# DVE's sorting step cut in two: the rows' places first, the blocks' experts and biases as a step of their own

## The chip, the cores and the metric

The kernel runs on one core of one Trainium2 chip. The metric is device microseconds (us) of one execution, lower is better. A core has five engines with a queue of instructions each: PE (matrix products), DVE (vector work), ACT (activations and copies), POOL (here it issues indirect DMAs, one for each 128 rows) and SP (here it issues all other DMAs). An engine runs its instructions in order, and engines meet in semaphores: an instruction that waits holds up all that stand behind it on its engine.

## The reference

Eight graphs of 1024 nodes with 128 features pass four residual layers, each behind a layer norm:

```python
x = x + _L0_gnn_ref(adj, _layernorm(x), W, b)         # maximum over up to 25 neighbours, then a product
x = x + _L0_ffn_ref(_layernorm(x), ...)               # 8 experts of width 512, the best 2 of each node
x = x + _L1_gnn_ref(_layernorm(x), adj, ...)          # masked attention, 8 heads of 16
x = x + _L1_ffn_ref(_layernorm(x), ...)               # 6 experts, the best 2 of each node

gate_logits = xf @ Wg + bg                            # _L0_ffn_ref, the layer that the change touches
top_w, top_i = jax.lax.top_k(gate_logits, 2)
top_w = softmax(top_w)
for e in range(E):
    h = gelu(xf @ W1[e] + b1[e])
    out = out + w_dense[:, e:e + 1] * (h @ W2[e] + b2[e])
```

## The kernel before

**Passes.** The kernel is a software pipeline over graphs. A pass works on up to four graphs at once, each in another stage: `att` (attention over keys and values, and the second expert layer) on graph g, `unit` (scores of the attention) on g+1, `near` (the neighbour product and the first expert layer) on g+2, `load` (finding and gathering neighbours) on g+3, and the loading and norm of g+4. Passes run from g = -4 to 7; the passes g = 0 to 3 are one loop and have all five parts, pass 4 has all but the last, pass 5 has no `load`.

**Order.** Each pass is planned at build time by `schedule`: steps such as `("dest",)` or `("find", 2)` stand in threads (`chain`), wait for others (`gate`), and cost what the table `COURSE` says. The planner takes the step that can start first and writes one list; each engine then runs its part of each step in the order of that list. So a changed cost or a new step can move steps of every engine.

**The sorting step.** In `near`, each node's two best experts are found on DVE (step `cha 0`, function `two_best`), PE counts ranks (`rank`), and DVE's step `dest` (function `places`, L1137) turns ranks into the place of each row in an order sorted by expert (`dest`, written at L1164), and then works out which expert each of 23 blocks of 128 sorted rows belongs to (`block_at`, L1169 to L1173) and each block's first biases (`bias_of`, a view of the tile `mparts`, L1174 to L1184). The semaphore `bk` is raised by the last of them, at L1182. POOL's step `scatter` waits for `bk` at L924 and then issues 16 indirect DMAs (L930) that write rows of `xn` to their places in `xs_dram`; POOL goes on with the neighbour gathers of later tiles (`gather t`, L903). SP then loads the sorted rows (`xs`, into a part of `HB`), and PE runs the blocks (`xT`, `up`, `ut`, `dn`); `up` reads `block_at`, ACT's part of `ut` reads `bias_of`.

**Steps around it, in a loop pass.** On DVE: `chb 0` (weights of the two experts, L1200 to L1207, written to `wts`), `pmax 0` (maximum over gathered neighbours in `G`, L1053 to L1070), `wc 0` (copies the transposed weights to `WT`, L1216), `find 2` (neighbour indices of tile 2, L1021 to L1037), `fina 0 1` (copies a finished attention product to `tmp`, L1366), `ba 0` (adds the second bias, L1226), `mask 0` (L1331), `finc 0 1` (L1373, L1375). On PE: `st` (scores with the mask, L1691 and L1694) and `av` (values, L1705) alternate, ACT's exponential (L1491) lies between them; `wt 0` (L1604) needs `wts`, `b 0` (L1614) needs `WT`, `finb 0 1` (L1715) needs `tmp` of `fina 0 1`. Later on PE and DVE: `s t h`, the score maxima of the next graph (PE L1670, DVE L1337). SP's step `stack 0` (L855) loads twelve slices of 128 KB once the attention step `st 1 0 7` is done; `load_adj` (L835) brings a tile of the adjacency matrix to `adj_sb`, which `deg` on ACT (L1409), `class` on PE (L1543) and `find` on DVE read.

Of the kernel before, what the change touches and what calls it, by code (L numbers as in the profile page):

```python
# [68 lines left out]
    "finb": [("PE", 0.5)], "finc": [("DVE", 0.9)], "projt": [("PE", 0.5), ("ACT", 0.6)], "projm": [("PE", 1.0)],  # L69
# [4 lines left out]
    "ye": [("ACT", 0.7)], "ys": [("SP", 5.0)], "scatter": [("POOL", 24.0)], "collect": [("POOL", 12.0)],  # L74
    "mix": [("DVE", 2.4)], "load_x": [("SP", 14.0)], "again": [("SP", 6.0)], "store_x": [("SP", 4.0)], "load_adj": [("SP", 5.0)],
# [42 lines left out]
def planned(att, unit, near, load, ahead):  # L118

    p = Plan()  # L120
# [24 lines left out]
    if near:  # L145
        if not unit:
            p.threads.append([("bias",)])
            p.gate(("gT",), ("bias",))
        p.chain([("gT",), ("gnn",), ("gnn_add",), ("lnv", 1), ("sq", 1), ("ln", 1), ("t0",), ("lg0",), ("cha", 0),
                 ("ex", 0), ("chb", 0), ("wt", 0), ("wc", 0), ("b", 0), ("ba", 0)])  # L150
        p.chain([("cha", 0), ("rank",), ("dest",)])
        p.threads[-1].pop(0)
        p.gate(("chb", 0), ("dest",))
        p.threads.append([("load_res",)])
        p.gate(("load_res",), ("take",) if unit else None)
        p.gate(("gnn_add",), ("load_res",))
# [88 lines left out]
    if near:  # L245
# [12 lines left out]
        blocks = [("xT", 0)]  # L258
# [95 lines left out]
def signals(step):  # L354

    k = step[0]
# [69 lines left out]
        return A("rank") + [("mk", ("cha", 0), 1)]  # L426
    if k == "dest":
        return [("bk", step, 1)]
    if k == "xs":
        return [(f"xl{step[1] % 2}", step, 16)] + ([("sca", ("scatter",), 16 * 2 * TILES)] if step[1] == 0 else [])  # L430
    if k in ("xT", "up", "ut"):
# [66 lines left out]
def graph_kernel(nc, x, adj, gW, gb, Wg, bg, W1, b1, W2, b2, Wq, Wk, Wv, Wo, bo,  # L498
                 rw1, rb1, rw2, rb2, ew1, eb1, ew2, eb2, ew3, eb3, out):
    ctx = ExitStack()  # L500
    with ctx:
# [3 lines left out]
        def sem(name):  # L505
# [32 lines left out]
        dest = sb("dest", [P, 2, TILES], U32)  # L538
        block_at = sb("block_at", [1, QUADS * HTILES], I32)
        counts = [sb(f"counts{i}", [P, EP]) for i in range(3)]  # L540
# [105 lines left out]
            "dg": "degree_excess_ready", "cat": "degree_class_ready", "aggr": "aggregate_ready", "q1": "first_part_ready",  # L646
            "parts": "parts_ready", "pd": "parts_stored", "stack0": "stacks_loaded0", "stack1": "stacks_loaded1",
            "dl": "router_input_ready", "ed": "router_exp_ready", "wts": "expert_weights_ready",
            "mk": "choices_marked", "bk": "sorted_places_ready", "sca": "rows_scattered",
            "xl0": "sorted_rows_loaded0", "xl1": "sorted_rows_loaded1", "yst0": "outputs_stored0",  # L650
            "yst1": "outputs_stored1", "col0": "outputs_collected0", "col1": "outputs_collected1",
            "mp": "max_parts_ready", "ms": "max_rows_stacked", "out": "stored"}.items()}
# [28 lines left out]
        def at(ps, turn, name, key=None):  # L681


            return S[name], reached(ps, turn, name, key)
# [9 lines left out]
        def is_free(ps, turn, key):  # L694


            name, v = ring_place(ps, turn, key)
            return free[name], v - 1
# [269 lines left out]
        def _(dve):  # L968
            def settle(ins):

                dve.drain()  # L971
                return ins
# [164 lines left out]
            def places(ps, turn):  # L1137
# [9 lines left out]
                for d in (1, 2, 4):  # L1147
# [3 lines left out]
                upto = src  # L1151
# [3 lines left out]
                ins = dve.scalar_tensor_tensor(out=spot, in0=need.unsqueeze(1).to_broadcast([P, TILES, EP]),  # L1155
                                               scalar=float(P), in1=ranks[:, 0:TILES, :], op0=ALU.mult, op1=ALU.add)
# [4 lines left out]
                dve.drain()  # L1161
                row = tmp[:, 3 * TILES * EP:3 * TILES * EP + 2 * TILES].rearrange("p (i t) -> p i t", i=2)
                settle(dve.tensor_reduce(out=row, in_=both, axis=AX.X, op=ALU.add))
                settle(dve.tensor_copy(dest[:, :, :], row))  # L1164
                B = QUADS * HTILES
                block_e = tmp[:, 2 * B * EP:2 * B * EP + B]
                own = tmp[:, 0:B * EP].rearrange("p (j e) -> p j e", e=EP)
# [10 lines left out]
                for c in range(HC):  # L1178
                    settle(dve.tensor_tensor(some, own, biases[:, c:c + 1, :].to_broadcast([P, B, EP]), ALU.mult))
                    ins = dve.tensor_reduce(out=cols[:, c, :, :], in_=some.rearrange("p (k j) e -> p k j e", k=PARTS),  # L1180
                                            axis=AX.X, op=ALU.add)
                    if c == HC - 1:  # L1182
                        ins.then_inc(S["bk"], 1)
                    dve.drain()  # L1184

            def mix(ps, turn, h):
# [94 lines left out]
            def body(ps, turn, b):  # L1281
                for step in ps.steps:
                    kind = step[0]
# [22 lines left out]
                        add_biases(ps, turn, step)  # L1306
                    elif kind == "dest":
                        places(ps, turn)
                    elif kind == "mix":
                        mix(ps, turn, step[1])  # L1310
                    elif kind == "acc1":
# [21 lines left out]
                    elif kind == "s":  # L1333
# [3 lines left out]
                        ins = dve.tensor_tensor_reduce(out=junk, in0=psum(ps, step)[:, :], in1=mask[:, t, :],  # L1337
                                                       scale=1.0, scalar=LOWEST, op0=ALU.add, op1=ALU.max,
                                                       accum_out=MX[:, h, t:t + 1])
                        ins.then_inc(*emptied(ps, step))  # L1340
                        dve.drain()
                    elif kind == "mparts":
# [5 lines left out]
                        for k in range(PARTS):  # L1348
                            ins = dve.tensor_copy(mparts[:, k, 0:HEADS * TILES], mrest[:, :])
# [6 lines left out]
                    elif kind == "mc":  # L1356
                        dve.wait_ge(*is_full(ps, turn, ("mT",)))
                        ins = dve.tensor_copy(mT[:, :, :].rearrange("p k n -> p (k n)"),
                                              psum(ps, ("mT",))[:, :].bitcast(BF16)[:, 0:PARTS * P])
# [19 lines left out]
                    elif kind == "proja":  # L1379
# [4 lines left out]
                        ins = dve.tensor_tensor(res_f[:, htiles[qh], :], res_f[:, htiles[qh], :], y, ALU.add)  # L1384
# [134 lines left out]
        def _(pe):  # L1519
# [17 lines left out]
            def body(ps, turn, b):  # L1537
                for step in ps.steps:
# [88 lines left out]
                    elif kind == "xT":  # L1627
                        q = step[1]
                        pe.wait_ge(*at(ps, turn, f"xl{q % 2}", ("xs", q)))
                        pe.wait_ge(*is_free(ps, turn, step))  # L1630
                        for r in range(HTILES):
                            ins = pe.transpose(psum(ps, step)[:, r * P:(r + 1) * P], xrows[q % 2][:, r, :], ident[:, :])
# [158 lines left out]
```

## Time and profile before

| | |
|---|---|
| Median of 3 runs | 3017.85 us (3013.54 to 3019.1) |
| The profiled execution | 3021.74 us |
| Its span in the profile | 3019.7 us |
| Granted TensorE clock, mean over the span | 0.869 |
| Busy: PE, DVE, ACT, POOL | 71%, 59%, 45%, 37% |

The span is what the engines' records cover; the execution's own time is 2.0 us longer. All places below are in us from the start of the span. The sorting step of the pass g begins at 237.5 (g = -2), 473.6 (-1), 726.0 (0), 1051.1 (1), 1375.1 (2), 1696.3 (3), 2042.8 (4) and 2341.7 (5), so a pass takes some 320 to 350 us. No engine is busy all the time: the time is made by waits between engines, and has to be read from the chain of work in each stretch.

### The profile page before, as it was taken

What the parts mean: (1) busy time and instruction counts of PE and PEld (TensorE: products, weight loads), DVE (VectorE), ACT (ScalarE), POOL (GpSimd) and SP (SyncE); (2) the same over time, 40 slices, a digit from 0 to 9 for tenths busy, and PEclk for the clock granted to TensorE, in tenths of its full rate; (3) what the DMA queues carried; (4) which work ended last, traced back from release to release, by engine and by line L of the source; (5) the groups of instructions that cost most, each with busy time, mean ns of one, the idle gap of its engine ahead of it and who ended that gap; (6) DMA issues with size and microseconds to landing.
All of it is one profiled execution on the core that took longest, in us unless ns stands there. A gap on an engine that the chain in (4) does not pass through costs nothing.

```text
span 3019.7 us, 46125 instructions
## 1 busy us (share of the span) xinstructions
PE 2140.1 (71%) x13857; PEld 1222.8 (40%) x13857; DVE 1792.6 (59%) x5240; ACT 1351.5 (45%) x2490; POOL 1116.7 (37%) x1207
## 2 busy tenths in 40 slices
PE   0012622868689777888688856988689979887796
PEld 0011511534345434544355424554355445443343
DVE  5335156877478746875578646875587357427503
ACT  1102511536455645455455634465455435542263
POOL 3747647545632373137512653237512200200000
PEclk9985855879889988999799987989899979988797
DMA  5635836644742466225722484235622221121000
GB/s 167 80 62 98 84 84 132 106 98 76 116 73 66 94 96 107 53 84 97 117 50 86 83 122 57 57 98 95 111 46 61 50 56 42 52 47 31 22 1 7
DMA packets 177922, 231.20 MB, mean 77 GB/s; under 512 B 27327, under 2 KB 123996, under 8 KB 177628
## 3 DMA queue, kind: packets, MB, share of 16 engines
q0 software_dynamic: 33536, 68.75, 22.1%
q1 hardware_dynamic: 144092, 159.02, 18.6%
q8 instruction: 125, 2.05, 0.3%
q14 instruction: 169, 1.38, 0.1%
HBM read 183.76 MB, written 43.52 MB: 75 GB/s over the span
## 4 chain that ended last, share of the span: by engine, by line
DVE 37%; PE 26%; issue 18%; DVEq 5%; DMA 5%; POOL 4%; ACT 2%; SPq 2%; POOLq 0%; ACTq 0%
DVE tmp L1337 15%; PE PY L1705 5%; PE PA L1691 5%; PE PA L1694 5%; DVE G L1053 3%; POOL G L903 3%; DVE res_f L1238 2%; DVEq L971 2%; DMA HB<-xs_dram 2%; PE PA L1670 2%; DVE score L1021 2%; DMA adj_sb<-in_adj 1%; DVE top L1025 1%; SPq L855 1%; PE PH L1642 1%
## 5 line engine op out<-in xcount | busy, mean ns | idle before, releaser
L903 POOL DMA_INDIRECT G<-table,slot_idx x792 | 819.9, 1035 | 262.0 <-issue 258.9
L1491 ACT ACTIVATE HB<-PA 128x1024 f32<-128x1024 f32 x512 | 500.1, 1022 | 404.5 <-PE PA L1694 386.8
L1337 DVE CUSTOM_DVE_ANT_0 tmp<-PA,mask 128x1024 bf16<-128x1024 f32 x512 | 626.5, 1224 | 90.9 <-issue 90.8
L1691 PE MATMUL PA<-QS,KS 99*128 99x512 bf16 x1024 | 418.6, 409 | 57.8 <-ACT HB L1491 20.0
L1670 PE MATMUL PA<-KS,QS 96*128 96x512 bf16 x1024 | 342.6, 424 | 156.6 <-DVE MX L1337 99.8
L747 POOL TENSOR_TENSOR pool_pad<-pool_pad 1x1 f32<-1x1 f32 x143 | 28.0, 205 | 1123.3 <-DMA ys_dram<-HB 445.9
L1694 PE MATMUL PA<-identb,mask 128*128 128x128 bf16 x4096 | 422.1, 228 | 0.0
L1694 PEld LDWEIGHTS PA<-identb,mask 128*128 128x128 bf16 x4096 | 337.4, 103 | 141.1 <-issue 30.4
L1705 PE MATMUL PY<-HB,VS 128*32 128x512 f32 x2048 | 289.7, 640 | 1.1 <-ACT HB L1491 1.1
L743 DVE MEMSET dve_pad<- 1x1 f32 x668 | 39.3, 59 | 370.7 <-DMA G<-table,slot_idx 177.8
L1473 ACT ACTIVATE HB<-PH,mparts 128x128 f32<-128x128 f32 x736 | 210.2, 369 | 92.5 <-PE PH L1649 91.9
L1670 PEld LDWEIGHTS PA<-KS,QS 96*128 96x128 bf16 x1024 | 88.6, 103 | 377.1 <-DVE MX L1337 187.0
L1642 PE MATMUL PH<-W_sb,XT 128*128 x368 | 213.0, 666 | 23.4 <-ACT HB L1473 14.2
L1512 ACT ACTIVATE parts<-PH,bias_T 128x512 f32<-128x512 f32 x192 | 132.0, 688 | 194.4 <-PE PH L1754 119.8
L1659 PE MATMUL PY<-W_sb,HB 128*128 x1472 | 202.3, 282 | 5.7 <-ACT HB L1481 5.1
L1659 PEld LDWEIGHTS PY<-W_sb,HB 128*128 128x128 f32 x1472 | 193.5, 199 | 23.9 <-issue 13.4
L1398 ACT ACTIVATE HB<-PH 128x512 f32<-128x512 f32 x184 | 110.2, 599 | 207.4 <-PE PH L1642 206.9
L1691 PEld LDWEIGHTS PA<-QS,KS 99*128 99x128 bf16 x1024 | 103.9, 101 | 227.0 <-ACT HB L1491 117.5
L1409 ACT ACTIVATE edges<-adj_sb 128x1024 uint8<-128x1024 int32 x64 | 67.6, 1057 | 227.7 <-DMA adj_sb<-in_adj 227.7
L1543 PE MATMUL PH<-excess,ones 128*1 128x2 f32 x128 | 12.2, 165 | 220.7 <-ACT excess L1412 200.5
L1523 PE MATMUL PH<-ident,xn 128*128 128x128 f32 x256 | 47.0, 334 | 156.1 <-DVE bias_T L1290 65.3
L930 POOL DMA_INDIRECT xs_dram<-xn,dest x128 | 136.6, 1067 | 40.6 <-issue 40.6
(197 smaller groups left out, 3073.9 us busy)
## 6 DMA issues: line engine op xcount, KB each, us to landing
adj_sb<-in_adj SPq DMA_DIRECT2D x64, 512.0 KB
adjm<-in_adj SPq DMA_DIRECT2D x64, 512.0 KB
G<-table,slot_idx POOLq DMA_INDIRECT x792
HB<-xs_dram SPq DMA_DIRECT2D x48, 256.0 KB, 6.0
ys_dram<-HB SPq DMA_DIRECT2D x48, 256.0 KB, 2.6
parts_dram<-parts SPq DMA_DIRECT2D x16, 768.0 KB
QS<-parts_dram SPq DMA_DIRECT2D x96, 128.0 KB, 4.6
KS<-parts_dram SPq DMA_DIRECT2D x96, 128.0 KB, 6.7
```

The costliest lines, as they stand in the source:

```text
L903: pool.indirect_dma_start(G[:, t % 2, s, :], None, table, bass.IndirectOffsetOnAxis(slot_idx[:, t, s:s + 1], axis=0), bounds_check=ROWS - ...
L930: pool.indirect_dma_start(xs_dram, bass.IndirectOffsetOnAxis(dest[:, i, t:t + 1], axis=0), xn[:, t, :], None, bounds_check=SORTED - 1, oob ...
L1337: ins = dve.tensor_tensor_reduce(out=junk, in0=psum(ps, step)[:, :], in1=mask[:, t, :], scale=1.0, scalar=LOWEST, op0=ALU.add, op1=ALU.max ...
L1473: ins = act.activation(hid[j % 2][:, c * P:(c + 1) * P], psum(ps, step)[:, c * P:(c + 1) * P], ACT.Gelu, bias=bias_of[:, k, n:n + 1])
L1491: act.activation(HB[:, kc % 2, 2 * pr:2 * pr + 2, :], psum(ps, key)[:, :].rearrange("p (h q) -> p h q", h=2), ACT.Exp, scale=float(D) ** - ...
L1512: act.activation(HE[:, k, :], psum(ps, step)[:, :], ACT.Relu, bias=bias_T[:, col + e:col + e + 1]).then_inc(*emptied(ps, step))
L1642: pe.matmul(psum(ps, step)[:, :], rows, W1_sb[:, expert[j], :], start=True, stop=True).then_inc(*filled(ps, step))
L1659: ins = pe.matmul(psum(ps, ("yb", q))[:, r * C:(r + 1) * C], hid[j % 2][:, c * P:(c + 1) * P], W2_sb[:, expert[j], c, :], start=(c == 0), ...
L1670: ins = pe.matmul(psum(ps, step)[:, half[hf]], QS[0:SROWS, h, t * P:(t + 1) * P], KS[0:SROWS, h, half[hf]], start=True, stop=True)
L1691: pe.matmul(o, KS[0:SROWS + PARTS, h, kc * P:(kc + 1) * P], QS[0:SROWS + PARTS, h, half[qh]], start=True, stop=False)
L1694: ins = pe.matmul(o[:, qt * P:(qt + 1) * P], mask[:, qh * HTILES + qt, kc * P:(kc + 1) * P], identb[:, :], start=False, stop=(qt == HTILES ...
L1705: ins = pe.matmul(psum(ps, key)[32 * hh:32 * hh + 32, :], VS[:, kc, (D + 1) * (g * GH + hh):(D + 1) * (g * GH + hh) + 32], HB[:, kc % 2, h ...
```

## The change

`places` ends with the places and raises `bk` there. The rest becomes a function `block_experts`, run in a new step `blocks` with a semaphore `bl` of its own, which PE waits for before `xT 0`. The planner is told the two costs, 3.4 and 2.8 us, in place of 6.0, and that `blocks` comes behind `dest` and ahead of `xT 0`.

```diff
-    "y1": [("PE", 1.0)], "acc1": [("DVE", 1.25)], "rank": [("PE", 2.5)], "dest": [("DVE", 6.0)],
+    "y1": [("PE", 1.0)], "acc1": [("DVE", 1.25)], "rank": [("PE", 2.5)], "dest": [("DVE", 3.4)], "blocks": [("DVE", 2.8)],
...
-        p.chain([("cha", 0), ("rank",), ("dest",)])
+        p.chain([("cha", 0), ("rank",), ("dest",), ("blocks",)])
         p.threads[-1].pop(0)
+        p.gate(("xT", 0), ("blocks",))
         p.gate(("chb", 0), ("dest",))
...
+    if k == "blocks":
+        return [("bl", step, 1)]
...
-                settle(dve.tensor_copy(dest[:, :, :], row))
+                settle(dve.tensor_copy(dest[:, :, :], row).then_inc(S["bk"], 1))
+
+            def block_experts(ps, turn):
+
+                upto = counts[1][:, :]
                 B = QUADS * HTILES
...
                     if c == HC - 1:
-                        ins.then_inc(S["bk"], 1)
+                        ins.then_inc(S["bl"], 1)
                     dve.drain()
...
+                    elif kind == "blocks":
+                        block_experts(ps, turn)
...
                         pe.wait_ge(*at(ps, turn, f"xl{q % 2}", ("xs", q)))
+                        if q == 0:
+                            pe.wait_ge(*at(ps, turn, "bl", ("blocks",)))
```

The planner's order moves with it. On DVE, in the loop pass, this is what stands from the end of the places to the mask before (the loops over `c` and the other classes of `pmax` left out at the dots):

```order
L1164 CAST dest<-tmp 128x16
L1169 TENSOR_TENSOR tmp<-counts,block_no 128x192
...
L1200 TENSOR_SCALAR w1st<-ed 128x8
...
L1207 TENSOR_TENSOR wts<-pick 128x64
...
L1053 TENSOR_TENSOR G<-G 128x1536
...
L1216 COPY WT<-PH 64x128
...
L1021 SCALAR_TENSOR_TENSOR score<-adj_sb,countdown 128x1024
...
L1366 COPY tmp<-PY 128x512
L1225 REGISTER_ALU
L1226 TENSOR_TENSOR res_n<-res_n,PH 128x512 x2
L1330 REGISTER_ALU
L1331 TENSOR_SCALAR mask<-adjm,drop 128x1024
```

And this is the same place of the changed kernel (its lines stand 3 to 11 further on; L1176 is the first row of `blocks`):

```order
L1167 CAST dest<-tmp 128x16
...
L1207 TENSOR_SCALAR w1st<-ed 128x8
...
L1214 TENSOR_TENSOR wts<-pick 128x64
L1176 TENSOR_TENSOR tmp<-counts,block_no 128x192
...
L1223 COPY WT<-PH 64x128
...
L1056 TENSOR_TENSOR G<-G 128x1536
...
L1233 TENSOR_TENSOR res_n<-res_n,PH 128x512 x2
...
L1024 SCALAR_TENSOR_TENSOR score<-adj_sb,countdown 128x1024
...
L1375 COPY tmp<-PY 128x512
L1339 REGISTER_ALU
L1340 TENSOR_SCALAR mask<-adjm,drop 128x1024
```

So the weights (`chb 0`) now stand ahead of the blocks, `WT` (`wc 0`) ahead of the maximum over neighbours (`pmax 0`), and the bias addition (`ba 0`) ahead of `find 2` and `fina 0 1`, where it stood behind both.

On PE, in the loop pass, the transposition of the weights and the bias product stand among the attention steps. Before:

```order
L1604 MATMUL PH<-ident,wts 128x128
L1705 MATMUL PY<-HB,VS 32x512 x4
L1687 REGISTER_ALU
L1691 MATMUL PA<-QS,KS 128x512
L1694 MATMUL PA<-identb,mask 128x128 x4
...
L1608 REGISTER_ALU
L1614 MATMUL PH<-bias_diag,WT 128x512 x2
L1705 MATMUL PY<-HB,VS 32x512 x4
```

In the changed kernel:

```order
L1613 MATMUL PH<-ident,wts 128x128
L1716 MATMUL PY<-HB,VS 32x512 x4
L1698 REGISTER_ALU
L1702 MATMUL PA<-QS,KS 128x512
L1705 MATMUL PA<-identb,mask 128x128 x4
...
L1617 REGISTER_ALU
L1623 MATMUL PH<-bias_diag,WT 128x512 x2
L1716 MATMUL PY<-HB,VS 32x512 x4
```

The distance between the two is the same; both stand one pair of `av` and `st` earlier than before: `wt 0` behind `st 0 1 6` (before: `st 0 1 7`), `b 0` behind `st 0 1 7` (before: `st 1 0 0`). In the second half of the passes 0 and 4, the steps `s` of PE and DVE mostly stand one place earlier among the expert steps than before. In pass -1, `wc 0` and `ba 0` come ahead of `pmax 0`, and the step `s 0 0` moves from ahead of `find 2` to behind `pmax 0`. In pass -2 and 5 only the steps next to `blocks` move. POOL's order is the same everywhere, and SP's but for one exchange of two neighbours.

## Rows read from the trace of the kernel before

**Rows 1.** The page: the chain that ended last, by engine

```profile
DVE 37%; PE 26%; issue 18%; DVEq 5%; DMA 5%; POOL 4%; ACT 2%; SPq 2%; POOLq 0%; ACTq 0%
```

**Rows 2.** Waits, all passes: engine, line, releaser, us in total, times, longest

```profile
POOL pool_pad L747 <- DVE mparts L1180: 88.1, 7, 59.4
```

**Rows 3.** Timeline of POOL, pass 1: start, us, engine, line, operation, idle before

```profile
1054.61 1.00 POOL L903 DMA_INDIRECT G<-table,slot_idx  x1 [0.30 <-issue]
1060.23 0.18 POOL L747 TENSOR_TENSOR pool_pad<-pool_pad 1x1 f32<-1x1 f32 x1 [4.62 <-DVE mparts L1180]
...
1150.20 0.18 POOL L747 TENSOR_TENSOR pool_pad<-pool_pad 1x1 f32<-1x1 f32 x1 [12.38 <-DVE dve_pad L1070]
```

**Rows 4.** Timeline of DVE, pass 1, from the places to the second bias

```profile
1054.00 0.28 DVE L1164 CAST dest<-tmp 128x16 uint32<-128x16 f32 x1
...
1059.79 0.35 DVE L1180 TENSOR_REDUCE mparts<-tmp 128x24 f32<-128x192 f32 x1
...
1061.51 0.23 DVE L1207 TENSOR_TENSOR wts<-pick 128x64 f32<-128x64 f32 x1
...
1068.45 0.28 DVE L1216 COPY WT<-PH 64x128 f32<-64x128 f32 x1 [0.16 <-issue]
...
1075.62 0.69 DVE L1366 COPY tmp<-PY 128x512 f32<-128x512 f32 x1
1076.47 1.28 DVE L1226 TENSOR_TENSOR res_n<-res_n,PH 128x512 f32<-128x512 f32 x2 [0.16 <-issue]
```

**Rows 5.** Timeline of PE, pass 1, the steps `wt 0`, `b 0` and `finb 0 1`

```profile
1061.79 0.33 PE L1604 MATMUL PH<-ident,wts 128*128 128x128 f32 x1 [1.80 <-DVE wts L1207]
...
1068.79 2.08 PE L1614 MATMUL PH<-bias_diag,WT 32*128 32x512 f32 x4 [3.80 <-DVE WT L1216]
...
1079.06 0.65 PE L1715 MATMUL PH<-ident,tmp 128*128 128x128 f32 x4
```

**Rows 6.** Timelines of DVE and PE, the same place in pass 3, then in pass 4

```profile
1706.63 0.22 DVE L1207 TENSOR_TENSOR wts<-pick 128x64 f32<-128x64 f32 x1
1717.94 0.69 DVE L1366 COPY tmp<-PY 128x512 f32<-128x512 f32 x1
1713.90 2.08 PE L1614 MATMUL PH<-bias_diag,WT 32*128 32x512 f32 x4 [3.79 <-DVE WT L1216]
1724.17 0.66 PE L1715 MATMUL PH<-ident,tmp 128*128 128x128 f32 x4
2064.73 0.69 DVE L1366 COPY tmp<-PY 128x512 f32<-128x512 f32 x1 [0.37 <-PE PY L1705]
2071.54 0.66 PE L1715 MATMUL PH<-ident,tmp 128*128 128x128 f32 x4
```

**Rows 7.** Timeline of SP's queue, and of DVE and ACT where they wait, pass 1

```profile
1095.58 2.68 SPq L855 DMA_DIRECT2D QS<-parts_dram  x6
1108.89 17.51 SPq L835 DMA_DIRECT2D adj_sb<-in_adj  x2
1115.77 0.06 DVE L743 MEMSET dve_pad<- 1x1 f32 x1 [8.74 <-DMA G<-table,slot_idx]
1123.96 0.06 DVE L743 MEMSET dve_pad<- 1x1 f32 x1 [1.06 <-ACT degree_class L1420]
1138.92 1.06 ACT L1409 ACTIVATE edges<-adj_sb 128x1024 uint8<-128x1024 int32 x1 [4.81 <-DMA adj_sb<-in_adj]
```

**Rows 8.** Stretches of pass 1: us, busy of each engine, clock, DMA share, GB/s

```profile
1060.00:1063.00 3.00, 1.21 (x9) 0.29 (x9) 1.32 (x8) 1.08 (x2) 1.93 (x3) 1.00 0.13 29
1069.00:1072.00 3.00, 3.00 (x12) 0.49 (x12) 2.31 (x3) 0.00 (x0) 2.39 (x3) 0.50 0.16 46
1126.00:1129.00 3.00, 3.00 (x16) 0.78 (x14) 1.50 (x4) 1.24 (x2) 2.53 (x5) 0.56 0.75 31
1135.00:1138.00 3.00, 0.02 (x1) 0.00 (x0) 2.14 (x5) 0.00 (x0) 2.19 (x4) 1.00 0.91 199
```

**Rows 9.** Timeline of DVE, pass -1, the step `s 0 0`

```profile
489.23 1.22 DVE L1337 CUSTOM_DVE_ANT_0 tmp<-PA,mask 128x1024 bf16<-128x1024 f32 x1 [5.27 <-issue]
```

More of the change, by code:

```diff
@@ L648, in graph_kernel @@
             "dl": "router_input_ready", "ed": "router_exp_ready", "wts": "expert_weights_ready",
-            "mk": "choices_marked", "bk": "sorted_places_ready", "sca": "rows_scattered",
+            "mk": "choices_marked", "bk": "sorted_places_ready", "bl": "block_experts_ready", "sca": "rows_scattered",
             "xl0": "sorted_rows_loaded0", "xl1": "sorted_rows_loaded1", "yst0": "outputs_stored0",
```

## The prediction

> **What bounds the kernel now.** I read the page first, then the list of waits, then the timelines of POOL, DVE, PE and SP around the sorting step in every pass, and last the busy time by stretches. The chain that ended last is spread over all engines, 37% DVE, 26% PE, 18% with no releaser shown [rows 1]: no engine is the bound, so an edit is worth what it shortens of the chain in its stretch. The list of waits shows what the change is aimed at: POOL waited seven times for the last write of `mparts`, 88.1 us together [rows 2]. That sum misleads. One of the seven is 59.4 us long [rows 2], in pass 5, which gathers nothing, and where the sorted rows are not loaded before the last attention step. The other six add to 28.7 us. In pass 1, where POOL stops for 4.62 us, it ends gather 0 at 1055.61 and starts the scatter only at 1060.23 [rows 3]; DVE had the places at 1054.28 and spent 1054.28 to 1060.14 on the blocks [rows 4]. In pass -2 POOL was later than the signal and did not wait.
>
> What ends last behind it is the reader's main question. POOL itself has slack: in pass 1 it stands still for 12.38 us at 1150.20, for DVE's `pmax 2` [rows 3]. The stretch from 1050 to 1080 is DVE's, which has hardly a gap from the places to the second bias [rows 4], with PE stopping for it twice, 1.80 us for `wts` and 3.80 us for `WT` [rows 5]. From 1080 to 1095 PE and ACT set the pace of the attention steps. They release `stack 0` at 1095.58; behind its twelve loads SP issues `load_adj 5` at 1108.89 [rows 7]. DVE then waits for gather 1 until 1115.77 (8.74 us) and, two maxima later, until 1123.96 for the class of tile 5, which hangs on that load; the next adjacency tile lands at 1138.92 [rows 7]. PE's list has the class of tile 6 ahead of the last attention step, so `stack 1`, the sorted rows and the whole second half come behind it. So there are two strands that meet: gathers on POOL, and attention to `stack 0` to `load_adj` on PE and SP. In pass 1 the second is later by 1.06 us.
>
> **The change, part by part.** Added work: one semaphore and one wait of PE at `xT 0`, for a step that is done some 90 us earlier in a loop pass; its price is below what a row shows, nothing. No arithmetic and no DMA is added.
>
> *POOL.* With the signal at 1054.28 POOL starts when gather 0 is issued, at 1055.61: 4.62 us earlier in pass 1 [rows 3], and the gathers 1 to 3 with it. By the end of gather 3 POOL waits for DVE anyway.
>
> *DVE, loop passes.* `chb` and `wc` are exchanged with work of the same stretch, their sum is the same. `ba 0`, 1.28 us and a gap of 0.17 [rows 4], now stands ahead of `find 2` and `fina 0 1`. So `fina 0 1` starts at 1075.62 + 1.45 = 1077.07 and ends at 1077.76.
>
> *PE, loop passes.* `wts` is ready at about 1055.9 (5.86 us less than 1061.74), before `wt 0` is reached. `WT` is ready where `wts` used to be, about 1062.3, and not at 1068.73 [rows 4]: `b 0` starts 6.5 us earlier. But it stands one pair of `av` and `st` earlier, 2.9 us (from `wt 0` to `b 0` one pair passed: 1068.79 - 1061.79, less the stop of 3.80 and some 0.3 of the transposition itself [rows 5]). From `b 0` to `finb 0 1` were 10.27 us [rows 5], with that pair 13.2, so PE comes to `finb 0 1` at 1062.3 + 13.2 = 1075.5. There it now waits for `fina 0 1` until 1077.76, and goes on 1.3 us earlier than at 1079.06. The stall has moved: of 3.6 us that PE wins, 2.3 are given back to the copy that has become late.
>
> The other passes by the same sum: pass 0 wins 1.7 us and pass 2 wins 1.5 (their rows read as those of pass 1, with 3.88 and 3.65 us in place of 3.44 from the start of L1366 to L1715). In pass 3 `find 2` is short: L1366 starts at 1717.94, 6.23 us ahead of L1715 [rows 6], and the copy is still in time. There PE's own sum decides: `wts` was ready at 1706.85, `b 0` starts at 1707.4 in place of 1713.90, and 10.27 + 2.9 later is 1720.6, so 3.6 us are won. Pass 4 has 6.81 us between the two rows [rows 6], and by the same sum some 3.9. Together 1.7 + 1.3 + 1.5 + 3.6 + 3.9 = **12.0 us**.
>
> *Pass -1.* DVE waits there for the class of tile 2 whatever stands around. `s 0 0` used to run inside that wait; now it comes behind it: 1.22 us and its gaps, 1.4 [rows 9]. `wc 0` (0.28 and a gap) now runs in the wait. That is **1.0 us lost**, since the second half of that pass is DVE's. POOL's 3.8 us there are covered by its waits for `pmax`.
>
> *Passes -2 and 5.* In -2 POOL was busy with gather 0 until 252 and DVE ready at 246; POOL is the bound behind it: nothing. In 5 PE did not stop at `wt 0` or `b 0`: nothing. If the cover in -2 were gone, its price is one step of blocks, 5.86 us.
>
> *What the two strands make of it.* I let the second half inherit the gain of the later strand, PE and SP. The lead of the gathers over it grows from 0 to 3.3 us in passes 0 to 2. It can be worth something: while gathers ran, DMA engines were 75% busy and moved 31 GB/s, and once POOL's gathers ended, 199 GB/s at 91% [rows 8], so the tile that landed at 1138.92 lands earlier when gather 3 ends earlier. Bounds: nothing, and 3.3 us in each of three passes. I take nothing, because the tile before it keeps its company of gathers. The Trainium skill's page "DMA: Bandwidth & Descriptors", section "Issuing engines are not separate DMA queues", says that DMAs issued by different engines share the same DMA engines. By that, an earlier scatter is no extra bandwidth, and the gathers' head start relieves SP's loads only for as long as POOL is ahead; this trace agrees (the two rates above), and it leaves my sum at 12.0.
>
> *The clock.* PE's stop of 1.80 us left it at 2.4 GHz (1.00 in 1060 to 1063), the stop of 3.80 brought 1.2 GHz (0.50 in 1069 to 1072) [rows 8], and `b 0` took 2.08 us. In the changed kernel the stops are about 2.0 us at `b 0` and 2.3 at `finb 0 1`, between the two. Bounds: no cost, or that of one slow stretch, some 2 us in each of passes 0 to 2. I take none, since both are nearer to 1.80.
>
> *The order in the second half* of passes 0 to 4. It moves some 25 score steps by one place. Nothing is removed; DVE has as much to do. I take zero, with 1.5 us a pass either way.
>
> **Sum.** 3021.74 - 12.0 + 1.0 = 3010.7 us for an execution like the profiled one, 11.0 less. That execution is 3.9 above the median of the three runs, 3017.85, so on the median 3006.9; I say **3007**.
>
> **Rivals.**
> - *The scatter's whole wait comes back.* POOL's strand was the later one, since DVE waits 8.74 us for gather 1 [rows 7]. Then 28.7 us minus nothing, a time of 2989. For it: the longest single wait in the chain of the middle stretch is that one. Against it: behind it the class of tile 5 still ended last.
> - *Swallowed.* The second half starts earlier and ends as before, or the gain is lost in DMA order: within 6 us of 3018. For it: DVE, not PE, paces most of the second half. Against it: everything in there starts from `xT 0`.
> - *The clock falls at the new stop.* Passes 0 to 2 then lose about 2.0 each, 6 in all: 3013. The page "TensorE: Matmul & The Clock Gate" of the Trainium skill, section "What's actually happening", has the engine throttled by default and released by activity. By that, two stops close together can bring 1.2 GHz where each alone would not.
> - *Slower: score steps stand in the way of expert steps.* In the loop passes PE meets `s` one place earlier, and an `s` waits for DVE to free a bank, 1.3 us of work a step. If of the 25 moved steps in each of five passes every third holds the experts by 1.3 us, that is 5 x 8 x 1.3 = 52 us less what DVE would have waited for anyway; at a third of that, 17 us lost against 11 won, 3024. It decides from 2.2 us a pass on. Against it: two banks let PE run ahead, and DVE, not the experts, is last in most of that stretch.
>
> **How the numbers follow.** Chances: forecast 0.42 (2999 to 3012), the whole wait back 0.15, the clock 0.10, swallowed 0.18, slower 0.15. The likeliest is the forecast, 3007. The range runs from 2990, which leaves out half of the first rival, to 3019, which leaves out most of the last: 2 in 10. About 0.2%, or 6 us, is what a measurement of this kernel can tell from no change: faster than 3011.8 are the forecast, the first rival and a third of the clock's, 0.60; slower than 3023.9 is 0.11; within is 0.29.
>
> **What would show it.** POOL's wait before its first scatter is gone or under 1 us in passes -1 to 4. PE's `wt 0` waits for nothing, its `b 0` about 2 us. The transposition at L1715 (L1726 in the changed kernel's lines) waits some 2 us for the copy in passes 0 to 2 and not in 3 and 4. `stack 0` begins 1.3 to 1.7 us earlier behind the sorting step in passes 0 to 2 and some 3.7 in 3 and 4, and the passes shorten by that. It would be wrong if the gathers' landing sets `find 5`, if the time between `xT 0` and the pass's end changes by over 2 us, or if pass -1 loses more than 1 us.

## The result, and the profile of the changed kernel

| | before | changed |
|---|---|---|
| Median | 3016.16 us (3013.54 to 3019.1, 4 runs) | 2982.89 us (2975.27 to 2985.84, 4 runs) |
| Ratio | 1 | 0.9886 (95% interval 0.9864 to 0.9907) |
| The profiled execution | 3021.74 us | 2975.27 us |
| Its span; granted clock | 3019.7 us; 0.869 | 2973.2 us; 0.877 |

The change makes the kernel 33 us faster. The forecast was 11 us on the median, 3007, and the range ended at 2990: the direction was right, the size three times too small.

The page of the profile has the same picture as [rows 1], with DVE's share of the chain three points higher:

```profile
DVE 40%; PE 25%; issue 18%; DVEq 6%; DMA 4%; POOL 3%; ACT 2%; SPq 2%; ACTq 0%; POOLq 0%
```

The waits (engine, line, releaser, us in total, times, longest). The seven waits for `mparts` of [rows 2] have become one, in pass 5, which hides it. The second row is DVE's wait for gathered neighbours, 177.8 us in 26 times before; the third its wait for the class of a tile, 116.5 before.

```profile
POOL pool_pad L750 <- DVE dest L1167: 53.8, 1, 53.8
DVE dve_pad L746 <- DMA G<-table,slot_idx: 153.9, 25, 20.1
DVE dve_pad L746 <- ACT degree_class L1429: 108.8, 33, 14.6
```

POOL in pass 1 (timeline; the counterpart of [rows 3]). Gather 0 is issued, the scatter's mark at 1047.02 waits for nothing, and gather 1 begins at 1070.15, 24.8 us after the copy to `dest` (which starts at 1045.38). Before it began 29.7 us after that copy. All distances given below as "after `dest`" are counted from the start of this copy.

```profile
1045.99 1.00 POOL L906 DMA_INDIRECT G<-table,slot_idx  x1 [0.30 <-issue]
1047.02 0.18 POOL L750 TENSOR_TENSOR pool_pad<-pool_pad 1x1 f32<-1x1 f32 x1
...
1069.46 0.54 POOL L750 TENSOR_TENSOR pool_pad<-pool_pad 1x1 f32<-1x1 f32 x1
1070.15 1.04 POOL L906 DMA_INDIRECT G<-table,slot_idx  x1 [0.15 <-issue]
```

PE in the same place (timeline; [rows 5] before): `wt 0` without a wait, `b 0` with 1.97 us of it, and a new stop of 3.28 us at `finb 0 1`, for the copy that `ba 0` has pushed back.

```profile
1048.33 0.28 PE L1613 MATMUL PH<-ident,wts 128*128 128x128 f32 x1
...
1053.46 1.13 PE L1623 MATMUL PH<-bias_diag,WT 32*128 32x512 f32 x4 [1.97 <-DVE WT L1223]
...
1069.09 1.11 PE L1726 MATMUL PH<-ident,tmp 128*128 128x128 f32 x4 [3.28 <-DVE tmp L1375]
```

Behind that stop the clock is at 1.2 GHz for a stretch (windows of pass 1: us, busy of PE, PEld, DVE, ACT, POOL, then clock, DMA share, GB/s):

```profile
1069.40:1073.40 4.00, 4.00 (x24) 2.83 (x23) 1.24 (x3) 1.02 (x1) 3.22 (x5) 0.50 0.56 172
1073.40:1077.40 4.00, 4.00 (x31) 1.95 (x29) 0.00 (x0) 1.97 (x3) 3.08 (x4) 0.76 0.23 58
```

From `finb 0 1` to `stack 0` it now takes 19.5 us (1069.09 to 1088.56) where it took 16.5 [rows 5, 7]. So `stack 0` comes 43.2 us after `dest`, and came 41.6 us after it: on the strand of PE and SP, pass 1 has lost 1.6 us. And yet it is 10.9 us shorter. The timeline of DVE in the middle of pass 1, against [rows 7], says where:

```profile
1096.10 0.06 DVE L746 MEMSET dve_pad<- 1x1 f32 x1 [2.52 <-ACT degree_class L1429]
1100.03 0.06 DVE L746 MEMSET dve_pad<- 1x1 f32 x1
...
1109.10 0.06 DVE L746 MEMSET dve_pad<- 1x1 f32 x1 [0.77 <-ACT degree_class L1429]
```

The row at 1100.03 stands ahead of `pmax 1`. Before, it waited 8.74 us for gather 1; now it does not wait. And the class of tile 5 (1109.10), which hangs on a load of SP, is there 63.7 us after `dest`, where it was at 70.0. That load was issued at about the same place (53.6 us after `dest`, before 54.9), but has landed by 61.1, not 67.3. This is ACT's first use of it, and SP's queue:

```profile
1106.46 1.06 ACT L1418 ACTIVATE edges<-adj_sb 128x1024 uint8<-128x1024 int32 x1 [2.19 <-DMA adj_sb<-in_adj]
1088.56 3.93 SPq L858 DMA_DIRECT2D QS<-parts_dram  x6
1092.54 6.15 SPq L858 DMA_DIRECT2D KS<-parts_dram  x6
1098.97 12.57 SPq L838 DMA_DIRECT2D adj_sb<-in_adj  x2
```

The same two things stand in all the full passes. `pmax 1` ends 66.0 us after `dest` before and 59.7 now (means over passes 0 to 4), ACT takes up tile 5 after 66.5 and 62.1 us, and `find 5` on DVE, which stands behind `pmax 1` and needs the class of tile 5, begins after 70.4 and 65.4 us. The wait for gather 1 is not gone everywhere: in passes 3 and 4, where DVE comes to `pmax 1` earlier, it is still 9.24 and 5.20 us. So both strands moved, the gathers' by its head start and SP's with it, and the step `find 6` begins 2.8 to 11.8 us earlier, while `stack 0` moved by +0.2, +1.6, +2.6, -4.1 and -4.7. The passes 0 to 4 became 9.9, 10.9, 6.5, 12.4 and 4.4 us shorter, 44.1 us of the 46.5 between the two spans. (The medians differ by 33 us only: the profiled execution of the kernel before was 5.6 us above its median, that of the changed kernel 7.6 us below its own and the fastest of the four.)

### The profile page after: what moved, and what is told of

It reads as the page before. It is cut to its first block, busy times and chain, and to the rows that moved or that the text cites. A ratio compares the mean times of both kernels' runs of the same rounds, so it can differ in the third digit from the quotient of the medians.

```text
span 2973.2 us, 46125 instructions
## 1 busy us (share of the span) xinstructions
PE 2118.0 (71%) x13857; PEld 1217.5 (41%) x13857; DVE 1792.5 (60%) x5240; ACT 1350.3 (45%) x2490; POOL 1126.2 (38%) x1207
## 4 chain that ended last, share of the span: by engine, by line
DVE 40%; PE 25%; issue 18%; DVEq 6%; DMA 4%; POOL 3%; ACT 2%; SPq 2%; ACTq 0%; POOLq 0%
DVE tmp L1346 15%; PE PA L1702 4%; PE PY L1716 4%; PE PA L1705 4%; DVE G L1056 3%; DVEq L974 2%; POOL G L906 2%; DVE score L1024 2%; DVE res_f L1245 2%; PE PA L1681 2%; DVE top L1028 2%; DMA HB<-xs_dram 2%; SPq L858 2%; PE PH L1653 1%; PE PY L1670 1%
## 5 line engine op out<-in xcount | busy, mean ns | idle before, releaser
L906 POOL DMA_INDIRECT G<-table,slot_idx x792 | 829.2, 1047 | 261.9 <-issue 258.9
L1670 PEld LDWEIGHTS PY<-W_sb,HB 128*128 128x128 f32 x1472 | 193.5, 198 | 24.5 <-issue 13.4
## 6 DMA issues: line engine op xcount, KB each, us to landing
HB<-xs_dram SPq DMA_DIRECT2D x48, 256.0 KB, 3.1
ys_dram<-HB SPq DMA_DIRECT2D x48, 256.0 KB, 2.8
```

Of the source, the lines that this page charges most:

```text
L906: pool.indirect_dma_start(G[:, t % 2, s, :], None, table, bass.IndirectOffsetOnAxis(slot_idx[:, t, s:s + 1], axis=0), bounds_check=ROWS - ...
L1670: ins = pe.matmul(psum(ps, ("yb", q))[:, r * C:(r + 1) * C], hid[j % 2][:, c * P:(c + 1) * P], W2_sb[:, expert[j], c, :], start=(c == 0), ...
```

## The experiments

Shares of the time before are ratios to runs of the kernel before on the same chip. The chips differ by under 1% (the kernel before had medians from 3012 to 3038 us), so ratios are compared. A ratio carries some 0.003 of its own from chip to chip: the changed kernel has 0.9886 here and 0.9916 on another chip. Expectations given in us are meant for the first chip, where the kernel before takes 3017 us. Shifts within a pass are read from one profiled execution of each kernel.

### The signal alone, the order alone, idle work on POOL, `ba 0` put back

**The signal alone**, in the kernel before; the planner knows nothing of it:

```diff
-        return [("bk", step, 1)]
+        return [("bk", step, 1), ("bl", step, 1)]
...
-                settle(dve.tensor_copy(dest[:, :, :], row))
+                settle(dve.tensor_copy(dest[:, :, :], row).then_inc(S["bk"], 1))
...
-                        ins.then_inc(S["bk"], 1)
+                        ins.then_inc(S["bl"], 1)
...
+                        if q == 0:
+                            pe.wait_ge(*at(ps, turn, "bl", ("dest",)))
```

> The kernel before with one thing of the change: the signal for the scatter is raised at the copy into dest, a second signal at the end of the same step stands for the block experts, and TensorE waits for that second one at xT 0. The planner's costs and the order on every engine stay those of before, so ba 0 stays behind fina 0 1. Theory A (the gain comes through POOL: scatter and gathers 1 to 3 some 5 us earlier, with the transfers of gathers and SP's loads no longer in each other's way): the whole gain or more, 2960 to 2985 us; scatter about 4.6 us earlier after dest in passes 0 to 4, pmax 1 some 7 us earlier. Theory B (the gain comes of the planner's new order, wc 0 and ba 0 earlier and the score steps one place on): 3005 to 3016 us.

Measured: 0.9898 (0.9874 to 0.9923), which is 2987 us on the first chip, 2 us above theory A's range and far from B's. Without any step moved, this is the gain of the whole change within the noise.

**The order alone**: the changed kernel with `pool.wait_ge(*at(ps, turn, "bl", ("blocks",)))` ahead of the scatter.

> The changed kernel with one edit: the scatter waits for the signal of the later step (blocks) instead of that of dest. The order on every engine is that of after. The scatter then starts about 1 us later than in the kernel before, since chb 0 stands between dest and blocks. Theory A (POOL): the gain is gone, 3005 to 3030 us. Theory B (order): the gain stays, 2975 to 2995 us.

Measured: 1.0014 (0.9998 to 1.0029). The gain is gone. PE's lead is there as in the changed kernel (`finb 0 1` begins 24.2 us after `dest` in pass 1, 23.7 in the changed kernel and 25.1 before), and `b 0` is 6.8 us earlier than before, but neither is worth anything that shows. Gather 1 starts 1.0 us later here than before (30.3 and 29.3 us after `dest`), so a gain of a few us by PE could be hidden behind that; the gain of the whole change could not. Theory B falls.

**Idle work on POOL** behind the scatter:

```diff
+            def idle(much):
+
+                for n in range(much):
+                    pool.tensor_tensor(pool_pad[0:1, 2 * TILES + 4:2 * TILES + 5], ...)
+                    pool.drain()
...
                             bounds_check=SORTED - 1, oob_is_err=False).then_inc(S["sca"], 16)
+                idle(20)
```

> The changed kernel with 20 one-element additions, each with a drain, on POOL behind the scatter's last issue in every pass; nothing that is computed changes. The scatter keeps its early start, but gathers 1, 2 and 3 lose it (about 5 us: 20 times the 0.17 us of such an addition plus the drains). Theory A: most of the gain is lost, 3005 to 3025 us, as it came with the gathers. If the gain came with the scatter's own rows (xs and xT earlier), or of the order (theory B): 2980 to 2992 us.

Measured: 1.0101 (1.0073 to 1.0129), more loss than expected. The dose, the delay that the idle work makes, was larger than meant: the first drain stood still for 3.5 to 5.0 us, so gather 1 began 36.4 us after `dest` on the mean of passes 0 to 4, 11.9 later than in the changed kernel and 7.1 later than before. The scatter kept its early start (2.0 us after `dest` in pass 1), and that saved nothing.

**`ba 0` behind `fina 0 1`** again, by `p.gate(("ba", 0), ("fina", 0, 1))` in passes with attention.

> The changed kernel with one gate more in the planner: ba 0 comes behind fina 0 1 on DVE, as in the kernel before. Everything else of the change stays; PE's stop at finb 0 1 should shrink by the 1.45 us of ba 0 and by what the clock loses behind it. Theory A has two readings: if stack 0 comes earlier and hands that on, 2965 to 2978 us; if the gathers alone set the first half of a pass, 2978 to 2987 us. Theory B gives ba 0's place a part of the gain: 2990 us or more.

Measured: 0.9891 (0.9866 to 0.9917): the same as the changed kernel within the noise. PE's strand did move: `stack 0` came 40.1 us after `dest`, against 40.9 in the changed kernel (means of passes 0 to 4), but `find 5` did not follow, with 65.5 and 65.4 us. So PE's stop at `finb 0 1` and its clock cost nothing that shows here.

### Which gather it is

The same 20 idle additions ahead of gather 2, and ahead of gather 3 (in `search`, `if t == 2 and ps.near: idle(20)`, or 3).

> The changed kernel with the same 20 idle additions on POOL (9.8 us where they stood behind the scatter), now between gather 1 and gather 2, in the six passes that have both scatter and gathers; nothing that is computed changes. Theory C (the link is gather 1's landing, for which DVE waits ahead of pmax 1): gather 1 is as early as in the changed kernel, so at most some 15 us lost, 0.988 to 0.994 of the time before. Theory D (all of POOL's line counts, gathers 2 and 3 too): as with the idle work behind the scatter, 1.004 to 1.012 of the time before.

> The same idle work one gather later, between gather 2 and gather 3; nothing that is computed changes. Theory C: 0.988 to 0.993 of the time before. Theory D: 1.000 to 1.012, less than with the idle work ahead of gather 2 only by what POOL's later waits for DVE (4.0 us ahead of gather 5, 8.9 us ahead of gather 6 in pass 1) take up.

Measured: 1.0013 (1.0 to 1.0027) and 0.9983 (0.9972 to 0.9994). Both fall between the two theories, and the dose has to be read first. POOL in pass 1 of the first of them (timeline):

```profile
1117.63 0.18 POOL L899 TENSOR_TENSOR pool_pad<-pool_pad 1x1 f32<-1x1 f32 x1
1127.83 0.18 POOL L899 TENSOR_TENSOR pool_pad<-pool_pad 1x1 f32<-1x1 f32 x1 [10.02 <-issue]
1128.17 3.19 POOL L899 TENSOR_TENSOR pool_pad<-pool_pad 1x1 f32<-1x1 f32 x5 [0.15 <-issue]
1131.81 5.07 POOL L899 TENSOR_TENSOR pool_pad<-pool_pad 1x1 f32<-1x1 f32 x13 [0.45 <-issue]
1138.29 1.01 POOL L913 DMA_INDIRECT G<-table,slot_idx  x1 [1.41 <-issue]
```

Behind gathers the first drain took 10 us, and gather 2 came 19 us later than in the changed kernel, not 10 (65.7 and 46.5 us after `dest`, means of passes 0 to 4). Such 19 us cost 0.0127 of the time (1.0013 - 0.9886), some 38 us; the 18 us at gather 3 (83.7 and 66.2) cost 0.0097, some 29; but 12 us at gather 1 cost 0.0215, some 65. By the microsecond of delay, summed over the seven passes that have it (-2 to 4, one more than the expectations say), gather 1 costs 65 / 12 = 5.4 us and gather 2 38 / 19 = 2.0. Measured from the changed kernel's other ratio, 0.9916, these are 4.7 and 1.5. Pass -2 alone has some 15 us of the 38 and of the 29 (it took 251.5 and 251.2 us, and 234.3 to 238.2 in the two profiles of the changed kernel), so in the full passes gather 2 weighs still less. Gather 2's delay shows where it should, as DVE's wait ahead of `pmax 2`, at 1169.86 in pass 1 of that kernel:

```profile
1169.86 0.06 DVE L746 MEMSET dve_pad<- 1x1 f32 x1 [17.54 <-DMA G<-table,slot_idx]
```

In the same kernel SP's loads met fewer gathers, and ACT took up tile 5 after 58.8 us (62.1 in the changed kernel, mean of passes 0 to 4), though only POOL's work was edited: from its issue to ACT's first use this load took 6.5 us, and 9.7 in the changed kernel. So the faster loads are the gathers' doing.

**Gather 1 ahead of the scatter.** The idle work shows what a later gather costs; these show what a still earlier one gives. On POOL alone:

```diff
-                for step in ps.steps:
+                steps = list(ps.steps)
+                if ps.load and ps.near:
+                    steps.remove(("scatter",))
+                    steps.insert(steps.index(("gather", 1)) + 1, ("scatter",))
+                for step in steps:
```

> The changed kernel with POOL's order alone edited: the scatter stands behind gather 1 instead of ahead of it; DVE, PE, ACT and SP keep the order of the changed kernel. Gather 1 starts some 23 us earlier, POOL waits for dest nowhere, gather 2 starts when it did. Theory C: pmax 1 waits for nothing, and what is left of the link is gone: 0.975 to 0.987. Theory D (gathers 2 and 3 set the time, and they stay where they are): 0.985 to 0.991. A loss (over 0.993) would say that the scattered rows, 22 us later, are late for xs.

> As the one before, with the scatter behind gather 2: gathers 1 and 2 both some 22 us earlier, gather 3 where it was; the scatter would end near 90 us after dest, about when xs 0 is issued now. Theory C: as with the scatter behind gather 1, or worse where gather 2 has to wait for pmax 0. Theory D: another gain, 0.970 to 0.985. If xs waits for the scattered rows, over 0.990.

Measured: 0.9873 (0.9855 to 0.9892) behind gather 1, and 1.001 (0.9993 to 1.0027) behind gather 2. By the first alone one would say that the link is used up. The passes say otherwise: pass -1 took 280.0 us with it, and 252.3 to 259.5 in all the kernels above. There the steps of tile 2 hang on a load that comes late, and DVE stands 30.74 us for its class (timeline of pass -1):

```profile
513.92 0.06 DVE L746 MEMSET dve_pad<- 1x1 f32 x1 [30.74 <-ACT degree_class L1433]
```

Behind gather 2 pass -1 took 298.1 us and pass -2 251.4 (235.3 behind gather 1), and the passes 0 to 4 were no shorter than behind gather 1. What holds that load up in pass -1 I did not follow further.

### The full passes alone, and the changed kernel again

With `if ps.load and ps.att:` in place of `ps.near`, the scatter moves in passes 0 to 4 only.

> The changed kernel with the scatter behind gather 1 on POOL, but only in the five full passes (0 to 4); the pass ahead of them (-1), which took 26 us longer with that order, and the one before keep the order of the changed kernel. Theory D (the gathers' line no longer sets the time once gather 1 is early enough): 0.985 to 0.990, as the changed kernel. Theory C' (in passes 0 to 4 the early gather 1 still gains, and pass -1 hid it): about 26 us less than the run with the order in all passes, 0.977 to 0.982.

> As the one before, with ba 0 behind fina 0 1 on DVE as well. If with gather 1 out of the way TensorE's line sets the first half of a pass, the 1.45 us and the clock at finb 0 1 now count: 5 to 12 us less than the one before, 0.973 to 0.980. If not, the same within 3 us.

> The kernel before with the early signal alone (dest one step, planner's order untouched) and the scatter behind gather 1 in passes 0 to 4 on POOL. If the order of wc, b and ba has no part in it, within 0.002 of the changed kernel with the same POOL order; if b 0's stop of 3.8 us counts now, 0.002 to 0.005 above it.

> The changed kernel itself, as the measure on the same chip for the three beside it: 0.986 to 0.991 of the time before.

Measured, on one chip: 0.9816 (0.9791 to 0.9841), with `ba 0` later 0.9817 (0.9792 to 0.9841), on the signal alone 0.9849 (0.9823 to 0.9876), and the changed kernel again 0.9916 (0.9887 to 0.9945), just above what was expected of it. The first is 29 us faster than the changed kernel beside it (2977.65 and 3006.42 us), with gather 1 some 23 us earlier and gather 2 where it was (45.8 and 45.9 us after `dest`). So in the changed kernel the place of gather 1 still costs time. The place of `ba 0` gives nothing even now: 5 to 12 us were expected if PE's strand had become the later one. The third lies 0.0033 above the first, where the expectation puts a cost of `b 0`'s stop, but their intervals overlap; whether the planner's order has a small share is left open.

### The gather without the change, and the lead taken away exactly

So far signal, scatter and gather 1 had moved together wherever the time fell, or the change stood under the edit. Two kernels part them: the kernel before with the scatter behind gather 1 in passes 0 to 4 and nothing of the change, and the changed kernel with `idle(5)` behind the scatter.

> The kernel before, its step and its one late signal as they are, with the scatter behind gather 1 on POOL in passes 0 to 4. The signal of the whole step comes long before the scatter then asks for it. If what the change gave was gather 1's earlier start and nothing else of the signal, this kernel without the change has the same as the one with the early signal and this order: 0.983 to 0.988. If the early signal itself is needed (the scatter's rows, TensorE's wait, the steps behind), 0.990 or more.

> The changed kernel with 5 instead of 20 idle additions behind the scatter: about 5 us (the first drain's 3.5 to 5 us and four times 0.34 us), which puts gather 1 back where it stands in the kernel before, while scatter, planner's order and everything else are those of the changed kernel. If gather 1's start is the whole of the gain: 0.998 to 1.003. If other parts of the change have a share: 0.990 to 0.996.

Measured: 0.9838 (0.9809 to 0.9867) and 1.0038 (1.0016 to 1.0059). Moving gather 1 without the change gives at least what the change gives. In that kernel the scatter no longer stops for its signal either, so gathers 2 and 3 too start 6 us earlier than before. Taking away POOL's lead behind the scatter, and nothing else, takes away all of the gain; gathers 2 and 3 lose their lead with gather 1 here. The idle work was 6 to 7 us instead of 5, with 4.01 us in the first drain (POOL, pass 1), and gather 1 came 1.7 us later than before:

```profile
1079.87 0.54 POOL L930 TENSOR_TENSOR pool_pad<-pool_pad 1x1 f32<-1x1 f32 x1
1084.42 0.19 POOL L930 TENSOR_TENSOR pool_pad<-pool_pad 1x1 f32<-1x1 f32 x1 [4.01 <-issue]
1084.76 0.84 POOL L930 TENSOR_TENSOR pool_pad<-pool_pad 1x1 f32<-1x1 f32 x3 [0.15 <-issue]
```

DVE's wait for gather 1 is back in it, 12.37 us, and in the other kernel it is gone (DVE ahead of `pmax 1`, pass 1 of the one, then of the other):

```profile
1121.69 0.06 DVE L746 MEMSET dve_pad<- 1x1 f32 x1 [12.37 <-DMA G<-table,slot_idx]
```

```profile
1091.78 0.06 DVE L743 MEMSET dve_pad<- 1x1 f32 x1
```

Eight of the kernels in the order of gather 1's start, in us after `dest`, means of passes 0 to 4, read from the timelines of POOL, DVE, ACT and SP's queue ("load 5" is the time from the issue of tile 5's load to ACT's first use of it; "changed, scatter behind gather 1" is the run with that order in passes 0 to 4 only):

| Kernel | gather 1 starts | `pmax 1` ends | load 5 | ACT takes up tile 5 | `find 5` starts | ratio |
|---|---|---|---|---|---|---|
| before, scatter behind gather 1 | 1.0 | 57.1 | 6.8 | 57.8 | 61.4 | 0.9838 |
| changed, scatter behind gather 1 | 1.2 | 57.0 | 7.2 | 58.1 | 61.7 | 0.9816 |
| before with the signal alone | 23.7 | 58.6 | 9.4 | 63.4 | 66.8 | 0.9898 |
| changed | 24.5 | 59.7 | 9.7 | 62.1 | 65.4 | 0.9886 |
| before | 29.3 | 66.0 | 12.3 | 66.5 | 70.4 | 1 |
| changed, order alone | 30.3 | 67.8 | 12.7 | 65.2 | 72.7 | 1.0014 |
| changed, 5 idle | 31.0 | 68.8 | 13.4 | 64.1 | 72.7 | 1.0038 |
| changed, 20 idle | 36.4 | 72.6 | 11.2 | 62.0 | 76.4 | 1.0101 |

The start of `find 5` needs both `pmax 1` and the class of tile 5, and the ratio follows it through the whole table, within the 0.003 between chips: 0.0263 over 15.0 us, which is 5.3 us of time for each microsecond, about one in each full pass (the last row has lost some 9 us in pass -2 too). In the four rows at the top `find 5` begins 3.4 to 3.6 us after ACT takes up tile 5, so the class ends last there; in the three at the bottom it begins 3.8 to 4.9 us after the end of `pmax 1`, and tile 5's load mostly no longer counts; in the kernel before the two are level. So from before to changed the time fell because both moved. The load took 11.2 to 13.4 us in the four kernels where gather 1 starts 29 us after `dest` or later, 9.4 and 9.7 where it starts near 24, and 6.8 and 7.2 where it is out of the way.

## Why the prediction was right and wrong

- **POOL starts with the places: right.** The wait of 4.62 us in pass 1 is gone, and gathers 1 to 3 begin 4.9, 5.0 and 3.6 us earlier after `dest` in pass 1 (1070.15, 1091.8 and 1115.0 now).
- **DVE and PE up to `finb 0 1`: right but for pass 2.** `finb 0 1` was forecast 1.7, 1.3, 1.5, 3.6 and 3.9 us earlier in passes 0 to 4, and comes 1.8, 1.3, 0.3, 4.1 and 4.7 earlier. The stop at `b 0` was to be about 2.0 us and is 1.90 to 1.99. At `finb 0 1` it was to be 2.3 us in passes 0 to 2 and is 4.90, 3.28 and 5.87.
- **The clock: wrong in passes 0 to 2.** I took no cost since both stops were forecast nearer to 1.80 us than to 3.80; the one at `finb 0 1` came out longer. Behind it PE lost 1.9, 3.0 and 2.8 us on the way to `stack 0` (18.5, 19.5 and 19.4 us where it took 16.5), more than it had won. So the strand of PE and SP, of which 12.0 us were forecast, has `stack 0` only 4.5 us earlier over the five passes: 4.4 later in passes 0 to 2, 8.8 earlier in 3 and 4. The rival on the clock had its price about right (2.0 us a pass were forecast) and its consequence wrong, as the time did not hang on that strand.
- **Pass -1: not told by one profile.** 1.0 us of loss was forecast and 1.2 measured, but the same changed kernel took 253.5 us there in one profile and 256.0 in another.
- **"I let the second half inherit the gain of the later strand, PE and SP. [...] The lead of the gathers over it grows": this step failed**, with the reason behind it, that the tile's load "keeps its company of gathers". In the rows of before, the class of tile 5 ended 1.06 us after DVE was ready for it, and I took it for a strand of its own. But DVE, done with `find 4` at 1107.03, had stood 8.74 us for gather 1, and the load that the class hangs on had run from 1108.89 to 1121.3 with that same gather, not landed until 1115.7, beside it. The runs tie the length of this load to the gathers: 12.3 us before, 9.7 with the gathers 5 us earlier, 6.8 with gather 1 ahead of the scatter, 6.5 with gather 2 held back. So POOL's queue was behind both waits, and the two were no separate strands. Moving it by some 5 us took the wait ahead of `pmax 1` and made the load land 6.2 us earlier in pass 1. The order-only kernel, with PE's share alone, is at 1.0014; the signal-only kernel, with POOL's share alone, is at 0.9898. So the forecast had the direction right by luck: it counted on PE's share, which shows nothing, and put POOL's at nothing.
- **The rates that were to price the relief were misread.** "Once POOL's gathers ended, 199 GB/s" is not what [rows 8] show: in that stretch POOL is still busy for 2.19 us, and it issued gather 3 until 1137.6 (its stop of 12.38 us up to 1150.20 [rows 3] begins at 1137.8). High and low rates both occur while gathers run, and the last section shows more of them.
- **The rival "the whole wait comes back"** (2989, given 0.15) came nearest. It had POOL's strand as the one that counts; that the class still ended last in pass 1, its argument against itself, held no ground because the class's load hung on the gathers. 28.7 us less waiting on POOL gave 33 on the first chip, with an interval of 28 to 41 us, and 25 by the ratio on another chip, so the size agrees within the noise. Single steps moved by more than the head start: `find 6` by up to 11.8 us.
- **The order in the second half: right** as far as it can be told. The order-only kernel has it all, at 1.0014.

## What to carry to other kernels

When two strands end within a microsecond of each other, ask what each was slowed by: if the one's traffic holds up the other's load, moving the first moves both, and the second is no floor. That POOL stands still for 12 us later in the same pass did not make its work slack: 5 us of head start on it were worth the whole gain, and PE's share none that shows. To learn which of two strands counts, delay or advance each alone, and read the dose from the trace before dividing by it: the idle work here took about twice as long as meant.

An engine's queue has an order of its own to be tuned: the work whose user waits (gather 1) belongs ahead of work that is needed 60 us later (the scatter), and the kernels with the queue reordered in passes 0 to 4 alone are the fastest here (0.9816 with the split, 0.9838 without, with intervals that overlap). Where it is reordered matters: in pass -1 the same order cost 20 to 27 us.

## What the runs showed that I had not expected

- A drain on POOL after indirect DMAs does not end with the last issue: 3.5 to 5.6 us behind the scatter's 16, and 5.5 to 13.6 us behind gathers, in which nothing else of POOL runs.
- A stop of PE of about 2 us can go either way for the clock. At `b 0` the changed kernel stops for 1.90 to 1.99 us in each full pass; in passes 1 and 3 the clock fell behind it, in passes 0, 2 and 4 it stayed at 2.4 GHz. Before, stops of 1.44 to 1.80 us at `wt 0` left it up in all five passes, and stops of 3.79 to 4.07 us at `b 0` brought 1.2 GHz in all five. So choosing "nearer to 1.80 than to 3.80" was no safe way to price a stop in between. These are the windows of pass 1 of the changed kernel, up to the stop's end and behind it:

```profile
1051.00:1053.40 2.40, 0.48 (x6) 0.21 (x3) 1.99 (x5) 1.57 (x2) 1.79 (x3) 1.00 0.40 99
1053.40:1057.40 4.00, 3.94 (x19) 1.24 (x20) 2.27 (x3) 0.00 (x0) 3.39 (x3) 0.68 0.11 35
```

And this is pass 0 of the same execution, the stop (timeline) and the window behind it:

```profile
738.19 1.13 PE L1623 MATMUL PH<-bias_diag,WT 32*128 32x512 f32 x4 [1.97 <-DVE WT L1223]
738.10:742.10 4.00, 3.91 (x32) 1.75 (x32) 2.26 (x4) 0.76 (x1) 3.39 (x3) 1.00 0.14 40
```

- The DMA engines can be busy and move little, and a load beside gathers is slow out of proportion. The load of 512 KB for tile 5 took 12.4 us in pass 1 of before; the median of such loads in the changed kernel is 4.1 us from issue to landing. These are the four stretches in which it ran, in the kernel before:

```profile
1107.60:1111.60 4.00, 3.60 (x36) 1.45 (x28) 0.00 (x0) 2.75 (x3) 3.09 (x4) 1.00 0.78 114
1111.60:1115.60 4.00, 0.00 (x0) 0.00 (x0) 0.00 (x0) 0.00 (x0) 2.98 (x4) 0.93 0.90 207
1115.60:1119.60 4.00, 0.81 (x2) 0.28 (x3) 2.67 (x5) 0.00 (x0) 3.19 (x3) 0.50 1.12 96
1119.60:1123.60 4.00, 1.53 (x6) 0.37 (x5) 2.72 (x8) 1.85 (x6) 3.09 (x4) 0.50 0.83 42
```

In the last of them 42 GB/s took 83% of the engines' time, in the second 207 GB/s took 90%, while POOL issued gathers in both. What makes the difference is open.
